# First transfers over two queues, four weight products at a time in an attention's last step, and a projection split around the first expert tile

## The chip, the core and the metric

The kernel runs on one core of one Trainium2 chip. A core has five engines that run their own instruction streams side by side and wait for each other by semaphores: TensorE (PE in the profile, with its weight loads as PEld), VectorE (DVE), ScalarE (ACT), GpSimd (POOL) and SyncE (SP, which here only issues transfers). The metric is the device time of one execution in microseconds (us), the median of several.

## What is computed

Two layers of cross attention and mixture of experts in float32, on x of 2 x 512 rows of 256 numbers, with a context of 2 x 1024 rows:

```python
x = x + L0_xattn(layernorm(x), ctx, ctx, mask0)      # 16 heads of 16; Wq, Wk, Wv, Wo with biases
x = x + L0_ffn(layernorm(x))                         # 8 experts 256-512-256, gelu, the best one of each row
x = x + L1_xattn(layernorm(x), ctx, ctx, mask1)      # layer norms of q, k and v with gains
x = x + L1_ffn(layernorm(x))                         # 7 experts 256-704-256, silu, two of each row, and a shared one
```

The attention of a head is softmax(q k^T / 4 + mask) v. The masks leave all but the last keys open in a way that lets the kernel compute with 256 keys of a batch instead of 1024 where a check on the masks (`flags`) allows it. That check is made on the chip, in the first half of layer 0's attention.

## The kernel before

**Start.** `sp_start` and `act_start` issue the first transfers on two queues, SP's and ACT's. SP's are the first half of x (tile `X`), the two halves of mask 0 (1 MB each), the second half of x, two bias rows, and mask 1. ACT's are the small constants (`cols`), the key weights (`WP` 0), the two halves of the context (`CT`), the value weights and the query weights. `pe_start` projects the keys as soon as the context and the key weights are there (L359, eight matmuls), then the first two of four value blocks (L380); then it transposes the normalized rows of x (L354), which DVE (`statistics`, L412 and what follows) and ACT (L451) make; then it projects the queries (L359 again), counts the open keys (L502), and goes on to the scores. POOL fills `KT` with a constant (L607), ACT fills `QT` in four pieces, two of them ahead of its copy of the keys out of PSUM (L637).

**An attention** has eight steps (`STEPS`; a step is a batch of 512 queries and a group of four heads), each of four gaps. In a gap of step n PE makes two of the eight *weights products* of the step (L859, keys by queries, 32 x 512 a matmul pair), whose exponentials ACT takes (L1201, PX), and two *tops*, the score products of a later step (L849), of which DVE takes the row maxima (L1039). Between the gaps stand the outputs (L880, twice a step, weights by values), the transposition of the maxima (L868), which DVE adds to the queries (L1045), and the transposition of a finished output (L893), which DVE divides (L1051, L1053). Tops use three PSUM banks in turn (`m_claim`), weights products three others (`e_claim`): a product waits until the one three before it is read. `pe_beside`, `dve_beside` and `act_beside` put other work into named gaps. In step 0 DVE works off `key_counts_rest` (L520 to L534) for mask 0, a piece after each top; in steps 2 and 3 the same for mask 1. SP starts to load the experts' weights behind the branch on `flags`, which DVE writes at the end of step 3.

**The last step** (7) has no tops. PE's order in it is: products 0 and 1, a transposed output, products 2 and 3, outputs, the transposition of the normalized rows of batch 0 (L354, written by DVE at L447 in step 6), products 4 and 5, in layer 0 the routing logits (L1520), products 6 and 7, a transposed output, outputs, in layer 0 the ranks (L1598 to L1603), outputs. In step 6 DVE makes the rows' statistics, one piece after each top.

**From attention to experts.** After the ranks DVE computes the places of the rows (`places0`), POOL scatters them to a buffer in HBM (L1688, four of batch 0), and SP reads tile 0 from it (L1813). Meanwhile PE (`fast_pe`) projects layer 1's keys and values from the context (L380, eight products each) and transposes batch 1's attention output (`close1`, L354). `ffn0_pe` runs over 16 tiles: transposing the next tile's rows (L1716, copied by DVE at L1785), up (L1730), down of the tile before (L1743), and `beside(i)`. `beside(0)` projects batch 1's output (`project1`, L380, 3.62 us); DVE adds it (L1060) and makes the statistics of the second rows, all in its own `beside(0)`. Batch 1's ranks stand in tile 4, and tile 8 waits for the scatter of batch 1. After the tiles comes layer 1's attention with the same steps, then the shared expert (L1855, L1866) and the routed ones (L1946, L1961).

## Time and profile before

| | us |
|---|---|
| median of 3 executions | 538.05 (535.56 to 538.39) |
| the profiled execution | 537.39 |
| its span, first to last instruction | 536.2 |
| PE busy in it | 496.9 |
| DVE, ACT, POOL busy | 260.2, 200.7, 87.3 |
| mean granted clock of TensorE | 0.986 |

The span falls into the start (to 29 us), layer 0's attention (to 127), layer 0's experts (to 227), layer 1's attention (to 313), the shared expert (to 382) and the routed ones (to 528). A busy PE isn't a PE at its peak: a product that waits for a bank or streams through a quarter of the array counts as busy as well. So the page's shares tell which engine matters, and the timeline of a stretch tells what ends its waits.

### The profile page before, as it was taken

How to read it: one execution, taken by the hardware profiler on the slowest of the kernel's cores; microseconds unless marked ns; L12 is line 12 of the kernel's file. 1: busy time of each engine (PE TensorE's matmuls, PEld its weight loads, DVE VectorE, ACT ScalarE, POOL GpSimd, SP SyncE). 2: the span in 40 equal slices, each digit the busy share in tenths (PEclk: the TensorE clock that was granted, in tenths of full speed). 3: DMA queues.
4: the chain of work that ended last, by engine and by line, in shares of the span. 5: the costliest groups of instructions: out<-in, count | busy, mean ns of one | idle time of the engine just before them, and what ended most of it. 6: DMA issues, size and time to landing. Idle time of an engine off the chain costs nothing.

```text
span 536.2 us, 8761 instructions
## 1 busy us (share of the span) xinstructions
PE 496.9 (93%) x3261; PEld 367.5 (69%) x3261; DVE 260.2 (49%) x775; ACT 200.7 (37%) x415; POOL 87.3 (16%) x125
## 2 busy tenths in 40 slices
PE   0999999999888989999999989999899999999995
PEld 0456545646788979755465436756799999999994
DVE  6457798664337365496677833351422222222220
ACT  2445655461345643454746632220222222222221
POOL 3134400003002020020000000047012212211222
PEclk9997999998999998999999999999999999999999
DMA  8521006997113121047000030039687667766712
GB/s 307 173 58 41 2 1 220 367 372 213 39 40 119 52 88 31 27 157 230 2 1 0 2 119 0 1 88 389 209 269 253 201 197 244 247 200 204 247 15 32
DMA packets 43367, 73.13 MB, mean 136 GB/s; under 512 B 3537, under 2 KB 33713, under 8 KB 43316
## 3 DMA queue, kind: packets, MB, share of 16 engines
q1 hardware_dynamic: 34564, 61.26, 33.8%
q0 software_dynamic: 4336, 6.75, 5.8%
q10 hardware_dynamic: 4416, 4.47, 2.7%
q8 instruction: 29, 0.48, 0.4%
q14 instruction: 22, 0.18, 0.1%
HBM read 56.35 MB, written 14.51 MB: 132 GB/s over the span
## 4 chain that ended last, share of the span: by engine, by line
PE 72%; DVE 13%; DMA 6%; issue 4%; ACT 2%; another core or an unknown queue 2%; POOL 1%; ACTq 0%; POOLq 0%; DVEq 0%
PE PS L1946 16%; PE PS L1961 9%; PE PS L849 8%; PE PS L859 7%; PE PS L1855 5%; DVE W L1039 4%; PE PS L880 4%; PE PS L380 3%; PE PS L1730 3%; PE PS L1743 3%; PE PS L1866 3%; PE PS L359 2%; DMA CT<-in_ctxT 2%; PE PS L354 2%
## 5 line engine op out<-in xcount | busy, mean ns | idle before, releaser
L1039 DVE TENSOR_REDUCE W<-PS 128x2 f32<-128x512 f32 x128 | 83.9, 686 | 37.2 <-PE PS L849 36.5
L1946 PE MATMUL PS<-PR,W 128*128 128x128 f32 x836 | 96.5, 275 | 0.0
L1946 PEld LDWEIGHTS PS<-PR,W 128*128 128x128 f32 x836 | 94.9, 192 | 0.1
L849 PE MATMUL PS<-W 32*128 32x256 f32 x512 | 84.2, 407 | 2.6 <-DVE W L1039 2.1
L859 PE MATMUL PS<-W 32*128 32x512 f32 x256 | 84.9, 655 | 0.9 <-ACT W L1201 0.7
L849 PEld LDWEIGHTS PS<-W 32*128 32x128 f32 x512 | 55.6, 188 | 25.3 <-issue 11.5
L1961 PE MATMUL PS<-W,PR 128*128 x228 | 52.5, 380 | 0.8 <-ACT PR L2662 0.8
L2713 POOL DMA_INDIRECT out<-PR,slots x19 | 29.7, 1563 | 129.6 <-ACT PR L2662 126.5
L1201 ACT ACTIVATE PR<-PS 128x512 f32<-128x512 f32 x64 | 35.2, 595 | 35.8 <-PE PS L859 35.6
L1961 PEld LDWEIGHTS PS<-W,PR 128*128 128x128 f32 x228 | 41.9, 190 | 6.1 <-issue 1.2
L1201 ACT ACTIVATE W<-PS 128x512 f32<-128x512 f32 x64 | 34.8, 594 | 25.1 <-PE PS L859 24.9
L1982 DVE TENSOR_TENSOR PR<-PR,PS 128x512 f32<-128x512 f32 x19 | 13.1, 688 | 59.7 <-PE PS L1946 59.7
L1855 PE MATMUL PS<-XT,W 128*128 128x512 f32 x88 | 40.1, 596 | 0.0
L859 PEld LDWEIGHTS PS<-W 32*128 32x128 f32 x256 | 25.9, 186 | 15.2 <-issue 6.0
L1730 PE MATMUL PS<-PR,W 128*128 128x128 f32 x256 | 32.3, 280 | 0.0
L1730 PEld LDWEIGHTS PS<-PR,W 128*128 128x128 f32 x256 | 30.9, 197 | 0.3 <-issue 0.3
L1743 PE MATMUL PS<-W,PR 128*128 128x256 f32 x128 | 31.1, 383 | 0.0
L1855 PEld LDWEIGHTS PS<-XT,W 128*128 128x128 f32 x88 | 16.2, 190 | 16.5 <-issue 16.1
L1773 ACT ACTIVATE PR<-PS,b1c 128x128 f32<-128x128 f32 x64 | 18.2, 366 | 23.1 <-PE PS L1730 20.2
L1743 PEld LDWEIGHTS PS<-W,PR 128*128 128x128 f32 x128 | 23.0, 190 | 3.4 <-issue 1.0
L1866 PE MATMUL PS<-W,PR 128*128 128x256 f32 x96 | 22.9, 381 | 2.1 <-DVE PR L1900 1.2
L1866 PEld LDWEIGHTS PS<-W,PR 128*128 128x128 f32 x96 | 18.0, 190 | 9.9 <-issue 5.8
(274 smaller groups left out, 588.4 us busy)
## 6 DMA issues: line engine op xcount, KB each, us to landing
W<-in_rguT SPq DMA_DIRECT2D x19, 1408.0 KB
W<-in_L_ffn_W SPq DMA_DIRECT2D x16, 512.0 KB, 9.6
...
```

The source lines that it names most:

```text
L849: m = pe.matmul(PS[:, bank, q * FK:(q + 1) * FK], QT[r:r + 32, g, c:c + 128], KT[r:r + 32, g, b * FK:(b + 1) * FK], start=True, stop=True)
L859: pe.matmul(PS[:, bank, :], KT[r:r + 32, g, b * FK + kb * 128:b * FK + (kb + 1) * 128], QT[r:r + 32, g, 512 * b:512 * (b + 1)], start=True ...
L880: m = pe.matmul(PS[32 * j:32 * j + 32, 6, :], VV[:, 2 * b + kb, h * VW:h * VW + 32], PX[s % 2][:, 4 * kb + j, :], start=(kb == 0), stop=(k ...
L1039: dve.tensor_reduce(NM[:, s % 2, q:q + 2, c], PS[:, m_bank(use), :].rearrange("p (q n) -> p q n", q=2), AX, ALU.max).then_inc(sem("m_free" ...
L1201: act.activation(PX[s % 2][:, HEADS_W[k], :], PS[:, e_bank(use), :], ACT.Exp).then_inc(sem("e_free"), 1)
L1730: m = pe.matmul(PS[:, up_bank(i), j * 128:(j + 1) * 128], W[:, o:o + 128], XS0[:, i % 2, k, :], start=(k == 0), stop=(k == 1))
L1743: pe.matmul(PS[:, bk, 0:D], HT0[:, i % 2, j, :], W[:, o:o + D], start=(j == 0), stop=False)
L1855: m = pe.matmul(PS[:, 2 * (n % 2) + w, :], W[:, k * 2 * F1 + o:k * 2 * F1 + o + 128], XT[:, k, 512 * b:512 * b + 512], start=(k == 0), sto ...
L1866: m = pe.matmul(half(4 + t // 2, t), HS[:, n % 2, t * 128:(t + 1) * 128], W[:, o:o + D], start=(j == 0 and t % 2 == 0), stop=(j == NJ1 - 1 ...
L1946: m = pe.matmul(PS[:, bank, j * 128:(j + 1) * 128], W[:, o:o + 128], XS[:, r % 2, k, :], start=(k == 0), stop=(k == 1))
L1961: m = pe.matmul(PS[:, 6, 0:D], HT[:, r % 2, j, :], W[:, bass.ds(slot * SLOT + o, D)], start=(j == 0), stop=(j == NJ1 - 1))
L2713: ins = pool.indirect_dma_start(out, off, YO[:, r % 2, :], None, compute_op=ALU.add)
```

## The change

Five things are changed.

- **First transfers.** Both queues carry half of x, half of the context and one set of weights ahead of a half of mask 0. The query weights stand behind a half mask on ACT's queue. The filling of `KT` goes from POOL to ACT, and all four fillings of `QT` come later on ACT. DVE makes the statistics of x first. PE's first value blocks come behind the transpositions of x.
- **Key counts.** `key_counts_rest` of mask 0 goes from step 0 to step 1 (the condition in `start_fast_dve`).
- **Last steps.** In step 7 of both layers four products are made in gap 0 and four in gap 2; two of each four take banks of the tops' ring, which is idle then. Layer 1's rows turn in the rings too.
- **Rows' statistics.** In step 6 of layer 0 they go by pieces of 2, 2, 1 and 4 behind the gaps' tops, and batch 1's are split between tiles 0 and 1.
- **Layer 0's last projection.** `project1` goes from behind tile 0's up products to ahead of them: one half before tile 0's transposition, one half right after it. Batch 1's ranks and places go from tile 4 to tile 3. PE has a new wait for `ranked`.

```diff
-    ROUTINGS = ((0, 0, 4, E0, 2), (0, 4, 4, E0, 5), (1, 0, 8, E1, 7))
+    ROUTINGS = ((0, 0, 4, E0, 0), (0, 4, 4, E0, 5), (1, 0, 8, E1, 7))
...
+    ROWS_TURN, LOGITS = (7, 1), (7, 2)
+    ROWS_BEGUN, ROWS_PIECES = 0, (2, 2, 1, 4)
...
+    def weights_of(n, gap):
+
+        if n == STEPS - 1:
+            return range(2 * gap, 2 * gap + 4) if gap % 2 == 0 else ()
+        return (2 * gap, 2 * gap + 1)
...
+        for use, n in E_USES.items():
+            if use[0] == "weights" and use[2] == STEPS - 1 and use[3] % 4 > 1:
+                bank = (m_bank(f"rows{use[1]}_0_1") + use[3] % 4 - 1) % 3
+            else:
+                bank, turn = 3 + turn % 3, turn + 1
+            banks[use], before[use], last[bank] = bank, last.get(bank, 0), n
+        return banks, before
...
     def sp_start():
-        sp.dma_start(X[:, 0:4, :], x_v[:, 0:4, :]).then_inc(sem("x0"), 16)
-        mask0 = A["mask0"].rearrange("(q p) n -> p q n", p=128)
-        for i in range(2):
-            sp.dma_start(m0i[:, 2 * i:2 * i + 2, :], mask0[:, 2 * i:2 * i + 2, :]).then_inc(sem(f"m0_{i}"), 16)
+        sp.dma_start(X[:, 0:2, :], x_v[:, 0:2, :]).then_inc(sem("x0"), 16)
+        load_keys0(sp, 0)
+        sp.dma_start(WP[:, 1, :, :], A["L0_xattn_WvT"].rearrange("(k p) n -> p k n", p=128)).then_inc(sem("wp_1"), 16)
+        load_mask0(sp, 0)
         sp.dma_start(X[:, 4:8, :], x_v[:, 4:8, :]).then_inc(sem("x1"), 16)
...
         act.dma_start(cols[:, :, :], A["cols"]).then_inc(sem("col"), 16)
-        load_keys0()
+        act.dma_start(X[:, 2:4, :], x_v[:, 2:4, :]).then_inc(sem("x0"), 16)
+        act.dma_start(WP[:, 0, :, :], A["L0_xattn_WkT"].rearrange("(k p) n -> p k n", p=128)).then_inc(sem("wp_0"), 16)
+        load_keys0(act, 1)
+        load_mask0(act, 1)
+        act.dma_start(WP[:, 2, :, :], A["L0_xattn_WqT"].rearrange("(k p) n -> p k n", p=128)).then_inc(sem("wp_2"), 16)
...
-        preset_queries(0)
-        preset_queries(1)
-        for f in range(2):
-            act.wait_ge(*at(0, "k_ps", f + 1))
-            act.activation(CP[:, 0, f, :], PS[:, f, :], ACT.Identity, bias=cols[:, C_COMPACT, 2 + f:3 + f]
-                           ).then_inc(sem("compact"), 1)
+        for j in range(2):
+            preset(KT[:, 2 * j:2 * j + 2, :], C_MAX)
+        keys_compact(0)
         act.wait_ge(sem("stats"), NORMS[True]["x0_0"])
...
-        act.wait_ge(sem("consts"), CONSTS + 1)
         for r in range(2):
             spread(act, KT, 0, r).then_inc(sem("kt"), 16)
-        preset_queries(2)
-        preset_queries(3)
+        for j in range(2):
+            preset(QT[:, 2 * j:2 * j + 2, 0:512], C_MASK)
...
-        for f in range(2):
-            queries_compact(f, f)
+        queries_compact(0, 0)
+        for j in range(2):
+            preset(QT[:, 2 * j:2 * j + 2, 512:1024], C_MASK)
+        queries_compact(1, 1)
...
-        pe.wait_ge(*at(0, "wp_1", 16))
-        values_pair(0)
         pe.wait_ge(sem("consts"), CONSTS)
         pe.wait_ge(*at(0, "xn", 4))
         for k in range(2):
             turn4(2 + k, [XN[:, j, :] for j in range(4)], k).then_inc(sem("turned"), 1)
+        pe.wait_ge(*at(0, "wp_1", 16))
+        values_pair(0)
         pe.wait_ge(*compact(0, 1))
...
+        settle(v, dve.memset(VR[:, 0:4 * VT], 1.0))
+        settle(v, dve.memset(ones16[:, :], 1.0))
+        dve.wait_ge(sem("x0"), 32)
+        whole(statistics(v, "x0_0", [X[:, t, :] for t in range(4)]))
...
-        for i in range(2):
-            dve.wait_ge(sem(f"m0_{i}"), 16)
-            dve.tensor_scalar(mu0[:, 2 * i:2 * i + 2, :], m0i[:, 2 * i:2 * i + 2, :], 0.0, None, ALU.not_equal
-                              ).then_inc(sem("mu0"), 1)
+        mask0_ones(0)
         dve.wait_ge(*at(0, "turned", 2))
         dve.tensor_copy(XT[:, 1, 0:512], PS[:, 3, :]).then_inc(sem("xt"), 1)
+        mask0_ones(1)
...
+    def project_half_batch(use, before, wi, b, j):
+
+        if j == 0:
+            claim_both(use)
+            taken(6, before)
+            taken(7, before)
+        filled(6 + j, project_half(6 + j, j, wi, b))
...
             if (n, gap) == (7, 1):
-                turn_rows(1, 0)
+                pe.wait_ge(*at(1, "rows", 4))
+                turn_ring("rows1_0", rows_for(1, 0))
...
+        if n == STEPS - 1:
+            for k in weights_of(n, gap):
+                pe_weights(l, n, k)
+            return
...
-            late = counts_rest(v, s - 2) if s > 1 else key_counts_rest(v, 0, mc[0][:, 0, :], mt[0]) if s == 0 else iter(())
+            late = counts_rest(v, s - 2) if s > 1 else key_counts_rest(v, 0, mc[0][:, 0, :], mt[0]) if s else iter(())
...
+        new_values(0)
         turn_batch("close1", rows_for(0, 1))
+        new_values(1)
+        project_half_batch("project1", "close1", 3, 1, 0)
+        pe.wait_ge(sem("ranked"), 1)
         pe.wait_ge(sem("nk_raw"), 2)
         pe.wait_ge(sem("nv_raw"), 2)
...
-            elif i == 4:
-                ranks_pe(1).then_inc(sem("ranks"), 1)
...
         def beside(i):
-            if i == 0:
-                project_batch("project1", "close1", 3, 1)
-            elif i == 2:
+            if i == 2:
                 pe.wait_ge(*at(0, "rows", 8))
                 turn_batch("rows0_1", rows_for(0, 1))
+            elif i == 3:
+                ranks_pe(1).then_inc(sem("ranks"), 1)
...
+        ffn0_pe(MAIN, beside, mid, first_maxima, lambda: project_half_batch("project1", "close1", 3, 1, 1))
...
-            dve_step(0, s, v, late)
-            whole(late)
+            dve_step(0, s, v, rows if s == 6 else empty, ROWS_PIECES if s == 6 else None)
+            if s == 5:
...
+        dve_xt("close1", 1)
         whole(gates0(v, 0))
...
+        add_projected("project1", 1, 0)
...
         def beside(i):
             if i == 0:
-                add_projected("project1", 1)
-                whole(statistics(v, "rows0_1", rows_of(1)))
+                for j in range(2):
+                    dve.wait_ge(sem(f"free{6 + j}"), USES[6 + j]["project1"])
+                for _ in range(5):
+                    next(second_rows)
+            elif i == 1:
+                whole(second_rows)
             elif i == 2:
                 dve_xt("rows0_1", 1)
...
-            elif i == 4:
                 dve.wait_ge(sem("ranks"), 2)
...
+        values_taken(0)
+        act_xt("close1", (6,), 1)
+        values_taken(1)
```

`load_keys0(q, b)` now loads one half of the context on queue q, `load_mask0(q, i)` one half of mask 0, `preset` fills a part of `KT` or `QT`, `mask0_ones(i)` converts one half of mask 0, and `keys_compact(f)` and `values_taken(n)` are the loops of before, one turn each.

ACT's queue and engine from the kernel's start, before and then after. `cols` are the constants, `WP` weights, `CT` context, `W<-in_mask` mask 0:

```order
L629 DMA cols<-in_cols 128x28
L680 DMA WP<-in_L_xattn_WkT 128x2x256
L682 DMA CT<-in_ctxT 128x2x256 x2
L683 DMA WP<-in_L_xattn_WvT 128x2x256
L684 DMA WP<-in_L_xattn_WqT 128x2x256
L666 ACT_TABLE_LOAD
L666 ACTIVATE W<-W,cols 128x1024 x2
L637 ACTIVATE W<-PS,cols 128x512 x2
L451 ACTIVATE PR<-X,NW 128x256 x2
```

```order
L647 DMA cols<-in_cols 128x28
L648 DMA X<-in_x 128x2x256
L649 DMA WP<-in_L_xattn_WkT 128x2x256
L706 DMA CT<-in_ctxT 128x2x256
L709 DMA W<-in_mask 128x2x1024
L652 DMA WP<-in_L_xattn_WqT 128x2x256
L687 ACT_TABLE_LOAD
L687 ACTIVATE W<-W,cols 128x1024 x2
L692 ACTIVATE W<-PS,cols 128x512
L472 ACTIVATE PR<-X,NW 128x256 x2
L692 ACTIVATE W<-PS,cols 128x512
L663 ACTIVATE XT<-PS 128x512
```

Half of x, half of the context and a half mask are on this queue now, and the other weights and the first half of the context have left it.

DVE in steps 0 and 1 of layer 0, before and after. TENSOR_REDUCE W<-PS are the maxima of tops, and the rows with fsum belong to the key counts:

```order
L1039 TENSOR_REDUCE W<-PS 128x2
L526 TENSOR_TENSOR fsum<-fsum 128x1
L527 TENSOR_SCALAR fsum<-fsum 128x1
L1039 TENSOR_REDUCE W<-PS 128x2
L529 TENSOR_SCALAR fsum<-fsum 128x1
L530 TENSOR_TENSOR fsum<-fsum 128x1
L534 COPY fsum<-fsum 128x1
L793 COPY b1c<-PS 128x32
L794 COPY wgs<-PS 128x24
L1039 TENSOR_REDUCE W<-PS 128x2 x2
L1045 TENSOR_TENSOR W<-W,PS 128x512
```

```order
L1080 TENSOR_REDUCE W<-PS 128x2 x3
L541 TENSOR_SCALAR W<-W 128x256
L542 TENSOR_REDUCE fsum<-W 128x1
L1080 TENSOR_REDUCE W<-PS 128x2
L544 TENSOR_TENSOR W<-W 128x256
L545 TENSOR_REDUCE fsum<-W 128x1
L1080 TENSOR_REDUCE W<-PS 128x2
L547 TENSOR_TENSOR fsum<-fsum 128x1
L548 TENSOR_SCALAR fsum<-fsum 128x1
L1080 TENSOR_REDUCE W<-PS 128x2
```

The rows of before are from step 0, those of after from the end of step 0 and step 1; ahead of them step 0 has nothing but six maxima, two copies and two maxima.

PE in step 7 of layer 0, before and after. W 128x512 are the products (L859, now L887), 32x512 the outputs, WGC the logits:

```order
L859 MATMUL PS<-W 128x512 x2
L893 MATMUL PS<-ident,W 128x128 x4
L859 MATMUL PS<-W 128x512 x2
L880 MATMUL PS<-PR,VR 32x512 x4
L354 MATMUL PS<-ident,W 128x128 x8
L859 MATMUL PS<-W 128x512 x2
L1520 MATMUL PS<-WGC,XT 128x8 x8
L859 MATMUL PS<-W 128x512 x2
L893 MATMUL PS<-ident,W 128x128 x4
L880 MATMUL PS<-W,VR 32x512 x4
```

```order
L887 MATMUL PS<-W 128x512 x4
L921 MATMUL PS<-ident,W 128x128 x4
L908 MATMUL PS<-PR,VR 32x512 x4
L375 MATMUL PS<-ident,W 128x128 x8
L887 MATMUL PS<-W 128x512 x4
L1558 MATMUL PS<-WGC,XT 128x8 x8
L921 MATMUL PS<-ident,W 128x128 x4
L908 MATMUL PS<-W,VR 32x512 x4
```

Eight products that stood in four pairs stand in two fours, the second of them ahead of the logits.

PE from layer 1's new values to tile 1's up products, before and after. WP,CT are new keys or values, WP,XT is `project1`, ident,PR a tile's transposition and PR,W its up products:

```order
L380 MATMUL PS<-WP,CT 128x256 x8
L354 MATMUL PS<-ident,W 128x128 x8
L1716 MATMUL PS<-ident,PR 128x128 x4
L1730 MATMUL PS<-PR,W 128x128 x8
L380 MATMUL PS<-WP,XT 128x256 x8
L1716 MATMUL PS<-ident,PR 128x128 x2
L1730 MATMUL PS<-PR,W 128x128 x8
```

```order
L401 MATMUL PS<-WP,CT 128x256 x4
L375 MATMUL PS<-ident,W 128x128 x8
L401 MATMUL PS<-WP,CT 128x256 x4
L401 MATMUL PS<-WP,XT 128x256 x4
L1754 MATMUL PS<-ident,PR 128x128 x2
L401 MATMUL PS<-WP,XT 128x256 x4
L1754 MATMUL PS<-ident,PR 128x128 x2
L1768 MATMUL PS<-PR,W 128x128 x8
L1754 MATMUL PS<-ident,PR 128x128 x2
L1768 MATMUL PS<-PR,W 128x128 x8
```

`project1` has left the place behind the first up products, and its halves stand around the first transposition.

## Rows read from the trace of the kernel before

**Rows 1.** The page: busy time of each engine, its share, instructions.
```profile
PE 496.9 (93%) x3261; PEld 367.5 (69%) x3261; DVE 260.2 (49%) x775; ACT 200.7 (37%) x415; POOL 87.3 (16%) x125
```

**Rows 2.** Transfers by queue (q1 SP, q10 ACT) in 5-12 us: packets, MB, share.
```profile
q1 hardware_dynamic: 659, 2.09, 76.0%
q10 hardware_dynamic: 654, 0.62, 26.6%
```

**Rows 3.** ACT's queue in 0-5 us, in 0-11 us and in 11-13 us.
```profile
q10 hardware_dynamic: 340, 0.22, 13.8%
...
q10 hardware_dynamic: 819, 0.67, 18.8%
...
q10 hardware_dynamic: 351, 0.34, 51.5%
```

**Rows 4.** Timeline of the start: start, length, engine, line, what, [idle before].
```profile
12.88 5.30 PE L359 MATMUL PS<-CT,WP 128*128 128x512 f32 x8 [12.88 <-DMA CT<-in_ctxT]
...
20.03 1.06 PE L354 MATMUL PS<-ident,PR 128*128 128x128 f32 x8
...
21.97 1.95 PE L359 MATMUL PS<-XT,WP 128*128 128x512 f32 x4 [0.88 <-DVE XT L762]
```

**Rows 5.** Timeline of step 0, layer 0: PE waiting, the first and last key counts.
```profile
44.16 0.28 DVE L520 TENSOR_SCALAR W<-W 128x256 f32<-128x256 f32 x1
...
47.16 0.76 PE L849 MATMUL PS<-W 32*128 32x256 f32 x1 [0.63 <-DVE W L1039]
...
48.28 0.15 DVE L534 COPY fsum<-fsum 128x1 f32<-128x1 f32 x1
```

**Rows 6.** Stretches: length; busy PE, PEld, DVE, ACT, POOL; PEclk, DMA share, GB/s.
```profile
44.00:48.00 4.00, 3.12 (x24) 2.33 (x22) 3.83 (x11) 2.77 (x5) 0.00 (x0) 0.86 0.00 1
48.00:52.00 4.00, 4.00 (x21) 2.74 (x22) 2.72 (x8) 2.14 (x3) 2.27 (x11) 0.50 0.00 0
...
120.00:124.00 4.00, 4.00 (x23) 2.31 (x26) 1.24 (x7) 1.51 (x3) 0.00 (x0) 0.75 1.09 337
124.00:128.00 4.00, 4.00 (x31) 1.75 (x24) 2.01 (x14) 0.71 (x2) 0.00 (x0) 0.83 0.98 262
```

**Rows 7.** Starts of steps 0, 1 and 2, and last outputs of steps 3 and 4.
```profile
42.50 0.69 PE L859 MATMUL PS<-W 32*128 32x512 f32 x1
...
54.39 0.48 PE L849 MATMUL PS<-W 32*128 32x256 f32 x1
...
64.25 0.48 PE L849 MATMUL PS<-W 32*128 32x256 f32 x1
...
83.16 1.06 PE L880 MATMUL PS<-W,VR 128*32 128x512 f32 x8
...
91.23 1.07 PE L880 MATMUL PS<-PR,VR 128*32 128x512 f32 x8
```

**Rows 8.** Timeline of step 7, layer 0, on PE; the second L880 is the last outputs.
```profile
113.30 1.13 PE L859 MATMUL PS<-W 32*128 32x512 f32 x4
...
123.37 1.94 PE L880 MATMUL PS<-W,VR 128*32 128x512 f32 x8
...
125.53 1.07 PE L880 MATMUL PS<-W,VR 128*32 128x512 f32 x8
```

**Rows 9.** Timeline of PE at tiles 0 to 2, layer 0's experts.
```profile
136.62 0.41 PE L1716 MATMUL PS<-ident,PR 128*128 128x128 f32 x2 [1.61 <-DMA PR<-scratch_x]
...
139.74 3.62 PE L380 MATMUL PS<-WP,XT 128*128 128x256 f32 x16
...
149.06 0.41 PE L1716 MATMUL PS<-ident,PR 128*128 128x128 f32 x2 [1.85 <-DVE PR L1785]
```

**Rows 10.** Timeline: PE at tile 8's transposition.
```profile
172.85 0.44 PE L1716 MATMUL PS<-ident,PR 128*128 128x128 f32 x2 [1.36 <-DMA PR<-scratch_x]
```

**Rows 11.** Timeline of step 7, layer 1: products 4 to 6, and the shared expert's start.
```profile
307.80 1.13 PE L859 MATMUL PS<-W 32*128 32x512 f32 x6
...
313.10 3.70 PE L1855 MATMUL PS<-XT,W 128*128 128x512 f32 x8
```

123 lines of the change are left out of this document (64 added, 59 removed).

## The prediction

> **What bounds the kernel now.** I read the page's busy times and its last chain first: PE is busy for 93% of the span, DVE for half of it [rows 1]. So a change pays where PE itself gets shorter, or where it waits, and nothing that DVE, ACT or POOL do beside a working PE counts. Where PE waits is told by the timeline's idle times. The stretches touched by the change have five such places: the start, where nothing runs on PE until the context has landed at 12.88 us [rows 4]; step 0 of layer 0, where PE waits for DVE [rows 5] and then runs at half the clock [rows 6]; step 7, where PE makes its products in pairs with ACT behind them [rows 8]; tile 0 and 1 of layer 0's experts [rows 9]; and tile 8 [rows 10]. All later stages follow by semaphores, so a gain at one place is carried on unless a transfer with its own time is met.
>
> **First transfers.** In 5 to 12 us the two queues moved 659 and 654 packets, but 2.09 and 0.62 MB: they take turns by packets, and SP's are the mask's long ones of 4 KB against ACT's of 1 KB [rows 2]. ACT's queue was at 340 packets after 5 us and at 819 after 11, which is 80 packets/us beside the mask; when SP too had short packets, in 11 to 13 us, it moved 351, 175 packets/us [rows 3]. The skill says the same (the Trainium skill, DMA: Bandwidth & Descriptors, section Queues, rings and completion order: an engine takes turns between queue rows at packet granularity), and by this rule a context that stands behind or beside the mask gets a fifth of the bytes; the trace agrees, with 0.62 of 2.71 MB.
>
> After the change ACT has to move the constants (128 packets), half x, key weights and half context (256 each), 896 in all, as many as before, which took until 11.4 us, 1.3 us ahead of the landing at 12.7. The difference is what runs beside them: SP has 768 short packets and then 256 of the mask, where it had 512 short and 512 long. At about 4.6 us SP is through with 512, and ACT has some 300 (340 less 0.4 us at its pace) [rows 3]. SP's other 256 short ones take 256 / 175 = 1.5 us and take ACT to 555; the 256 long ones take 256 / 80 = 3.2 us, to 9.3, and take ACT to 811; the last 85 take 0.5 us, to 9.8. With 1.3 us to the landing the context is there at 11.1 to 11.2 instead of 12.7: 1.6 us. The nearest other row is 175 packets/us without any mask beside it, 3.4 us for the 596 packets left at 4.6: landing at 9.3; with both queues at full pace from their first byte it would be 7.6, 5.3 us of gain. I take 11.2, since SP does reach its mask before ACT reaches its end.
>
> The keys take 5.3 us from there [rows 4], to 16.5. Before, ACT normalized its rows of x only behind both copies of the keys, and PE made two value blocks (1.9 us) meanwhile. Now the normalizing stands between the two copies: keys' first half done at 11.2 + 3.6, copy 0.7, rows 1.1, so the rows are there at 16.6 and PE transposes them at 16.7 instead of 20.03 [rows 4]. The value blocks come next (1.9) and hide the two copies of the transposed rows (0.6 + 0.7). The first queries start at 19.65 instead of 21.97 [rows 4]. The query weights stand behind a half mask on ACT's queue: 256 long and 256 short packets after 9.8 us are 3.2 + 1.5 us, landing near 16, in time. ACT's fillings of `QT`, two of 1.09 us, fit between 19.3 and the first queries' end at 21.6, and two more end 0.3 us ahead of the second queries. DVE's `mask0_ones` (1.2 each) is done by 19.7, ahead of the counts. So **2.3 us** go, between 1.6 (the keys alone) and 6.
>
> **Steps 0 and 1.** Step 0 lasts from 42.5 to 54.39, 11.9 us [rows 7]. Its counts take DVE 2.3 us between 44.16 and 48.43 [rows 5], 0.6 us of it between two maxima, so the three banks of tops run dry and PE waits; then it goes at half the clock, 1.2 GHz: all of 48 to 52 us and, by the mean of 0.86, the last 1.1 us ahead of it [rows 6]. Steps without counts show what it could be: the last outputs of steps 3 and 4 start 8.07 us apart [rows 7]. Step 0 has neither outputs of a step before (1.07) nor a transposed output (0.5), but a small job (0.5): 7.1 us. ACT's own work in it is 8 x 0.55 + 2 x 1.05 = 6.5. I take 7.7, a gain of 4.2. The counts now stand in step 1, which lasts 9.9 us [rows 7] with DVE at 6.9; 9.2 of 9.9 is tight, and step 2, which has counts and a division on DVE, is 0.9 us longer. I charge 0.9. Net **3.3 us**; if the clock falls all the same, 1.0.
>
> **Step 6.** The last top's maximum has two statistics ahead of it instead of three (0.35 us): **0.3 us**.
>
> **Step 7 of layer 0.** From 113.30 to the end of the last outputs at 126.6 it lasts 13.3 us [rows 8]. A pair of products takes 1.13 us, and in layer 1's step 7 three take 1.13 as well [rows 11], since each uses another quarter of the array's rows; four I put at 1.2. The new order by durations: products 1.2, transposed output 0.5, outputs 1.05, then the rows (written by DVE at 116.2) 1.05, to 117.25; products 1.15, logits 1.9, to 120.3; transposed output 0.6, outputs 1.05; ranks, for which DVE's six small operations (1.3) must be done at 121.6; outputs 1.07: 123.3 at full clock. ACT has 8 x 0.55 + 2 x 0.6 = 5.6 us between 114.5 and 120.1 and isn't late for the outputs. The skill warns of that (the Trainium skill, TensorEngine Tiling (Array Packing), section PSUM Bottleneck: once row tiles speed up the products, copying out of PSUM may bound); by it the step would be ACT's 5.6 us plus what stands ahead and behind, which still ends ahead of 123.3 here. Before, outputs took 1.94 instead of 1.07 late in the step [rows 8], with the clock at 1.2 GHz for some 3.4 us of 120 to 128 [rows 6], behind the logits. The logits stay, so I assume that this comes again, 1.3 us: **2.0 us** go, 3.3 without it, 0 if the fours go no faster than pairs.
>
> **Tile 0.** The places follow the ranks, the scatter the places, the read the scatter, so tile 0 lands 2.0 us earlier too: near 134.6 where PE took it at 136.62 after 1.61 us of waiting [rows 9]. PE's path from the step's end at 124.6 is: new keys 3.6, transposed output 0.5, half the values 1.8, `close1` 1.0, the other half 1.8, half a projection 1.8 (half of 3.62 [rows 9]): 135.1. So the waiting is filled. Then the first transposition 0.4, the other half 1.8, the second transposition 0.4: tile 0's up at 137.7, hardly earlier than before (138.0), but with no projection behind it. Tile 1's up stands at 139.9 instead of 143.4. The statistics, 4.3 us on DVE ahead of the copy for which PE waited 1.85 us [rows 9], are now 1.8 ahead of one copy and 2.4 ahead of the next, beside PE's 3.7 and more per tile, so that wait goes as well: tile 2's up at 144.0 instead of 149.3. That is 5.3 us, of which 2.0 are step 7's; with 0.3 for copies that come late once, **3.0 us**. DVE's new wait for the ranks in tile 3 has only the copy of tile 5 behind it, which PE asks for 4 us later. The wait for `ranked` ends with the places, 9 us ahead of PE's coming to it.
>
> **Tile 8.** Batch 1's places come some 2 us further ahead by their own move, so that the read of tile 8 lands at its own pace ahead of PE: **1.4 us** [rows 10], 0 if not.
>
> **Step 7 of layer 1.** From 302.9 to 313.10 [rows 11]. By the same durations: products 1.2, 0.5, outputs 1.05, rows 1.1, products 1.2, 0.6, then outputs at 308.8, and the last at 309.9, when ACT's eighth exponential is done (308.0 + 4 x 0.55 less its start): shared work starts at 311.0. **2.1 us**. The chain behind it (DVE, POOL's scatter) starts from PE's work and shifts along.
>
> **Sum.** 2.3 + 3.3 + 0.3 + 2.0 + 3.0 + 1.4 + 2.1 = 14.4 us. The profiled execution took 537.39, so 523.0 for one like it; the median shown is 538.05, 0.66 above, which gives 523.7. I say **523.4**.
>
> **The rivals.** (A) The mask doesn't hold up the context, since ACT's queue gets going before 4 us: the start gives 6.0 instead of 2.3, so 519.7. For it: 1 KB packets at full pace need only 5 us. Against it: rows 2. Chance 0.15; with it I put the case that the clock's fall in step 7 doesn't come again, 522.1 alone.
> (B) Step 0 keeps its wait or its half clock, the small job then being what holds PE: 2.3 us less, 525.7. For it: POOL and the two copies stand in the same gap; against: DVE would have only 5.8 us of work in 7.7. Chance 0.2.
> (C) The fours don't do what they say, since the banks borrowed from the other ring come free late: steps 7 give nothing, 4.1 us less, 527.5. Against it: three at once in rows 11. Chance 0.08.
> (D) The expert loads and the buffer's zeroing start with the branch and come only 5.6 us earlier, while the scatter comes 7.6 earlier and runs into the end of a backlog that kept the transfers' share near 1 until 128 us [rows 6]; tiles 0 and 8 then give 1 instead of 4.4: 526.8. Chance 0.1.
> (E) Slower: PE falls to half the clock more often. Two stretches of this attention spend over 5 and 3.4 us at 1.2 GHz [rows 6]. If thinner waits left it there through steps 1 to 6 (58 us, all PE), it would need 14.4 / 0.5 = 29 us at half clock to eat the gain; all of it would give 552. Chance 0.02.
>
> **How the numbers follow.** The forecast has 0.45. Its own terms move by the start (516 to 524) and by the clock. The range 516 to 529.5 takes in A to D and the bounds of each term. What a measurement of this kernel can tell from no change is about 0.5%, 2.7 us: only E and a sum of B, C, D and the low end of the start reach above 535.4. Faster 0.95, same 0.02, slower 0.03.
>
> **What would show it.** First keys at 11.2, first queries near 19.7, first top of step 1 near 48.8 with the granted clock at full through it; last outputs of step 7 some 7.6 us earlier; no idle time ahead of tiles 0, 2 and 8; layer 1's step 7 at 8.1 us. The prediction is wrong if the context lands after 12.5, if maxima still hold PE in step 0, or if ACT ends its exponentials after PE wants the outputs.

## The result, and the profile after

The changed kernel took 522.55 us (median of 4 runs, 519.58 to 523.77) against 537.82 us (4 runs, 535.56 to 538.39) of the kernel before: a ratio of 0.972, 95% interval 0.967 to 0.977. 523.4 us was predicted, with a range of 516.0 to 529.5. The profiled execution's span went from 536.2 to 522.5 us, by 13.7 us. The page of the changed kernel begins so, where [rows 1] stands before it:

```profile
PE 490.4 (94%) x3259; PEld 366.3 (70%) x3261; DVE 259.0 (50%) x776; ACT 201.1 (38%) x416; POOL 85.8 (16%) x124
```

PE is busy 6.5 us less and waits 7.2 us less. Where that is, the timelines of both traces tell: the start of the same piece of work in either, in us, with the shift that the prediction's terms had added up to by then.

| Work of PE | before | after | shift | predicted |
|---|---|---|---|---|
| first product of tops | 29.45 | 26.98 | -2.5 | -2.3 |
| step 1 of layer 0 | 54.39 | 48.14 | -6.3 | -6.5 |
| step 2 | 64.25 | 59.15 | -5.1 | -5.6 |
| step 7 | 113.30 | 108.03 | -5.3 | -5.9 |
| behind step 7's last outputs | 126.53 | 117.58 | -9.0 | -7.9 |
| tile 2's up | 149.30 | 136.73 | -12.6 | -10.9 |
| tile 7's up | 173.12 | 159.64 | -13.5 | -12.3 |
| step 7 of layer 1 | 302.92 | 289.42 | -13.5 | -12.3 |
| shared expert of layer 1 | 313.10 | 297.68 | -15.4 | -14.4 |
| first full up of a routed tile | 382.01 | 369.04 | -13.0 | -14.4 |
| last products | 527.68 | 514.03 | -13.7 | -14.4 |

So 15.4 us had been won by the shared expert, and 1.7 were given back behind it. Stretches in which PE's granted clock is 1.2 instead of 2.4 GHz have a part in this: ahead of the end, the trace of before has four times 1.7 us of such loss (twice in step 0, once in step 7, once at 200 us), that of the changed kernel two (at 187 and 364 us). So of the 13.7 us of this pair up to 3.4 are clock and at least 10.3 are not. The rows of the changed kernel's trace, in the order of the prediction's steps. First PE's timeline at the start (start, duration, then line, operation, count, and in brackets the idle time ahead and what ended it), which answers to [rows 4]:

```profile
10.98 6.40 PE L380 MATMUL PS<-CT,WP 128*128 128x512 f32 x8 [10.98 <-DMA CT<-in_ctxT]
17.22 1.04 PE L375 MATMUL PS<-ident,PR 128*128 128x128 f32 x8
19.82 1.88 PE L380 MATMUL PS<-XT,WP 128*128 128x512 f32 x4
26.98 1.14 PE L877 MATMUL PS<-W 32*128 32x256 f32 x8
```

The context is taken at 10.98 (11.2 predicted) and the first queries stand at 19.82 (19.65 predicted). The queues between 5 and 12 us, which answer to [rows 2] (packets, MB, share of the engines):

```profile
q1 hardware_dynamic: 663, 1.43, 52.9%
q10 hardware_dynamic: 696, 1.24, 47.5%
```

Again the two move the same number of packets, and now ACT's queue (q10) gets 1.24 MB of 2.67 instead of 0.62 of 2.71. Then step 0: PE's only wait in it, and the windows (PEclk is the granted clock, the third number from the end), which answer to [rows 5, 6]:

```profile
43.90 0.45 PE L877 MATMUL PS<-W 32*128 32x256 f32 x1 [0.37 <-DVE W L1080]
...
44.00:48.00 4.00, 4.00 (x36) 2.35 (x36) 3.10 (x8) 3.22 (x6) 2.46 (x12) 1.00 0.00 0
48.00:52.00 4.00, 4.00 (x36) 2.04 (x32) 3.24 (x8) 2.96 (x6) 3.42 (x12) 1.00 0.00 0
...
120.00:124.00 4.00, 4.00 (x26) 3.54 (x25) 1.59 (x4) 0.49 (x1) 3.09 (x4) 1.00 0.94 317
```

Step 0 lasts 8.1 us instead of 11.9, at full clock. Step 7 of layer 0, from its first four products to its last outputs, against [rows 8]:

```profile
108.03 1.14 PE L887 MATMUL PS<-W 32*128 32x512 f32 x8
...
112.93 1.95 PE L1558 MATMUL PS<-WGC,XT 128*128 128x8 f32 x16
114.74 0.64 PE L921 MATMUL PS<-ident,W 128*128 128x128 f32 x4
115.30 1.06 PE L908 MATMUL PS<-W,VR 128*32 128x512 f32 x8
...
116.59 1.06 PE L908 MATMUL PS<-W,VR 128*32 128x512 f32 x8
```

Eight records of 1.14 us in all are the four products (two matmuls each); a pair took 1.13 before. Tiles 0 to 2, against [rows 9]:

```profile
128.69 0.41 PE L1754 MATMUL PS<-ident,PR 128*128 128x128 f32 x2 [0.89 <-DMA PR<-scratch_x]
...
132.88 1.95 PE L1768 MATMUL PS<-PR,W 128*128 128x128 f32 x16
...
136.51 0.38 PE L1754 MATMUL PS<-ident,PR 128*128 128x128 f32 x2
```

Tile 1's up stands at 132.88, and the wait of 1.85 us for the copy is gone. Layer 1's step 7, against [rows 11], with a wait for ACT's exponentials at its end, and the place behind the shared expert where the late loss begins:

```profile
289.42 1.14 PE L887 MATMUL PS<-W 32*128 32x512 f32 x8
...
296.68 1.06 PE L908 MATMUL PS<-W,VR 128*32 128x512 f32 x8 [0.55 <-ACT W L1239]
...
363.36 0.92 PE L1906 MATMUL PS<-W,PR 128*128 128x256 f32 x3 [1.93 <-DVE PR L1940]
...
364.00:368.00 4.00, 4.00 (x14) 3.19 (x13) 1.49 (x6) 0.00 (x0) 0.00 (x0) 0.58 1.05 307
```

### The profile page after: what moved, and what is told of

Read it like the earlier page. It is cut to its first block, busy times and chain, and to the rows that moved or that the text cites. A ratio compares the mean times of both kernels' runs of the same rounds, so it can differ in the third digit from the quotient of the medians.

```text
span 522.5 us, 8762 instructions
## 1 busy us (share of the span) xinstructions
PE 490.4 (94%) x3259; PEld 366.3 (70%) x3261; DVE 259.0 (50%) x776; ACT 201.1 (38%) x416; POOL 85.8 (16%) x124
## 4 chain that ended last, share of the span: by engine, by line
PE 73%; DVE 12%; DMA 6%; issue 4%; ACT 2%; POOL 1%; ACTq 0%; SPq 0%; POOLq 0%; DVEq 0%
PE PS L1986 17%; PE PS L877 8%; PE PS L2001 8%; PE PS L1895 6%; PE PS L887 6%; PE PS L1906 4%; PE PS L908 3%; DVE W L1080 3%; PE PS L401 3%; PE PS L1768 3%; PE PS L380 3%; PE PS L1781 2%; PE PS L375 2%; DMA CT<-in_ctxT 2%; PE PS L896 2%
## 5 line engine op out<-in xcount | busy, mean ns | idle before, releaser
L887 PE MATMUL PS<-W 32*128 32x512 f32 x256 | 78.7, 638 | 0.2
L877 PEld LDWEIGHTS PS<-W 32*128 32x128 f32 x512 | 55.1, 184 | 24.8 <-issue 11.2
L887 PEld LDWEIGHTS PS<-W 32*128 32x128 f32 x256 | 24.0, 183 | 13.3 <-issue 6.6
L1781 PE MATMUL PS<-W,PR 128*128 128x256 f32 x128 | 31.0, 382 | 0.0
L1906 PE MATMUL PS<-W,PR 128*128 128x256 f32 x96 | 24.4, 399 | 2.9 <-DVE PR L1940 1.9
## 6 DMA issues: line engine op xcount, KB each, us to landing
W<-in_mask SPq DMA_DIRECT2D x2, 1024.0 KB, 12.6
```

The costliest lines, as they stand in the source:

```text
L877: m = pe.matmul(PS[:, bank, q * FK:(q + 1) * FK], QT[r:r + 32, g, c:c + 128], KT[r:r + 32, g, b * FK:(b + 1) * FK], start=True, stop=True)
L887: pe.matmul(PS[:, bank, :], KT[r:r + 32, g, b * FK + kb * 128:b * FK + (kb + 1) * 128], QT[r:r + 32, g, 512 * b:512 * (b + 1)], start=True ...
L1781: pe.matmul(PS[:, bk, 0:D], HT0[:, i % 2, j, :], W[:, o:o + D], start=(j == 0), stop=False)
L1906: m = pe.matmul(half(4 + t // 2, t), HS[:, n % 2, t * 128:(t + 1) * 128], W[:, o:o + D], start=(j == 0 and t % 2 == 0), stop=(j == NJ1 - 1 ...
```

## The experiments

Twelve more runs were made on three chips, of nine varied kernels and three repeats, each beside the kernel before on its own chip. Since stretches at 1.2 GHz turned out to come and go between executions of one kernel, the table takes them apart: "at half clock" is (1 - the mean granted clock of an execution) x its span, averaged over the runs; the rest, the mean time less that, is called the schedule here and set against the kernel before's on the same chip. The split is rough in three ways. A fall of the clock behind PE's last products is in every trace (0.2 to 1.7 us by this measure) and is taken off though it costs nothing. And a stretch inside counts in full though PE partly waits in it: the one in step 0 of the first trace of before counts 3.4 us, and the step is 2.6 us longer than in the second trace, which has none there. And the slow start of the keys (5.1 to 6.5 us until PE's next work, see the last section) isn't in the column, so it scatters the schedule.

| Kernel | runs | ratio to before (95%) | at half clock, us | schedule against before, us |
|---|---|---|---|---|
| before, on the three chips | 7, 13, 14 | 1 | 7.2, 7.4, 6.7 | 0 |
| changed, first | 4 | 0.972 (0.967 to 0.977) | 3.9 | |
| changed, again (after2) | 4 | 0.968 (0.965 to 0.971) | 1.4 | -10.9 |
| u_start | 4 | 0.979 (0.977 to 0.980) | 3.1 | -7.8 |
| u_counts | 4 | 0.973 (0.970 to 0.976) | 4.0 | -11.2 |
| u_pairs | 4 | 0.980 (0.977 to 0.983) | 3.4 | -7.4 |
| u_proj | 4 | 0.980 (0.976 to 0.985) | 4.4 | -7.7 |
| b_counts | 10 | 0.996 (0.993 to 0.998) | 4.2 | +1.0 |
| fours_only | 7 | 0.992 (0.989 to 0.995) | 7.2 | -4.8 |
| mask_last | 4 | 0.965 (0.962 to 0.969) | 2.1 | -13.4 |
| mask_last2 (the same) | 5 | 0.969 (0.966 to 0.973) | 2.2 | -12.3 |
| m_split | 6 | 0.970 (0.967 to 0.974) | 3.6 | -13.2 |
| m_counts0 | 6 | 0.974 (0.969 to 0.979) | 7.9 | -13.8 |

The schedule of one kernel's runs scatters by 0.4 to 1.6 us (standard deviation). With four to seven runs each, two entries of the last column differ clearly only when they are some 2 us apart on one chip, and more across chips. u_start, u_counts, u_pairs and u_proj ran on one chip; after2, mask_last and b_counts on the second; mask_last2, m_split, m_counts0 and fours_only on the third. So the undone kernels are best set against u_counts, whose only difference from the changed kernel leaves the schedule as it is in the traces (below): they are longer than it by 3.4, 3.8 and 3.5 us.

**The kernels once more.** after2 is the changed kernel, before2 the kernel before, both without an edit.

> The changed kernel once more, beside the others, to have its time and a second trace of it. If its steps are the program's, step 0 lasts 8.1 us, step 1 11.0, layer 0's step 7 9.5 and layer 1's 8.2, at full clock, as in the first trace; if they are one execution's, they differ. Open: whether PE again waits 1.93 us for the second to last chunk of the shared expert and then runs at 1.2 GHz for some 4 us, which cost 1.8 us in the first trace, and whether the stretch at 1.2 GHz behind the wait at 186 us comes again (2.3 us). With both it takes 0.9716 of the kernel before, without them 0.964.

> The kernel before once more, for a second trace. Theory (its falls of the clock are placed by its waits): 1.2 GHz again in step 0 behind the waits for DVE, in layer 0's step 7 behind the logits, and behind the wait for x1 at 200 us. Rival: only some of these places fall in any one execution, as the run with pairs, whose step 7 stayed at 1.00, lets suspect; then a second trace shows another set.

after2 took 519.46 us. Its trace has no stretch at 1.2 GHz ahead of the end, and the same distances: first tops at 27.32, last outputs of step 7 at 116.9 (0.3 behind the first trace in both). The wait behind the shared expert was 1.19 us. before2 took 537.37 us and had another set of stretches than the first trace. Its windows, columns as above:

```profile
36.00:38.00 2.00, 2.00 (x3) 0.74 (x3) 1.10 (x3) 0.00 (x0) 1.78 (x5) 0.50 0.08 26
48.00:50.00 2.00, 1.23 (x12) 0.80 (x7) 1.91 (x5) 1.72 (x3) 0.00 (x0) 1.00 0.00 0
122.00:124.00 2.00, 2.00 (x7) 0.54 (x4) 0.86 (x5) 0.44 (x1) 0.00 (x0) 0.50 1.09 336
126.00:128.00 2.00, 2.00 (x20) 0.49 (x16) 1.04 (x7) 0.00 (x0) 0.00 (x0) 0.50 0.97 328
```

Step 7 fell again and for longer, step 0 did not (PE waited in it the same 0.63 us for DVE, and the step took 9.3 us instead of 11.9), and there were stretches at 36, 241 and 309 us that the first trace hasn't. The starts of its step 0 and step 1:

```profile
45.40 0.69 PE L859 MATMUL PS<-W 32*128 32x512 f32 x1
...
54.67 0.48 PE L849 MATMUL PS<-W 32*128 32x256 f32 x1
```

So neither theory holds alone: step 7's is regular, the others come by chance, some more often than others.

**u_start: the first transfers undone.** All hunks of the diff from the order of transfers to DVE's start were put back; for instance

```diff
-        sp.dma_start(X[:, 0:2, :], x_v[:, 0:2, :]).then_inc(sem("x0"), 16)
-        load_keys0(sp, 0)
+        sp.dma_start(X[:, 0:4, :], x_v[:, 0:4, :]).then_inc(sem("x0"), 16)
+        mask0 = A["mask0"].rearrange("(q p) n -> p q n", p=128)
```

> The changed kernel with the order of first transfers, and of what ACT, DVE and PE do with them, put back as it was. Theory (the start's gain is real and carried to the end): the context lands at 12.7 to 12.9 us again, the first product of tops starts at 29.4 instead of 26.98, every later stage is 2.5 us later: 525.0 against 522.5. Rival (a later stage has a time of its own, so the start's gain would have been swallowed): the first tops at 29.4, but some wait later shorter by as much, 522.5.

It took 521.91 us against 533.54 of before. PE's timeline:

```profile
12.94 6.41 PE L380 MATMUL PS<-CT,WP 128*128 128x512 f32 x8 [12.94 <-DMA CT<-in_ctxT]
...
21.20 1.06 PE L375 MATMUL PS<-ident,PR 128*128 128x128 f32 x8
23.14 1.95 PE L380 MATMUL PS<-XT,WP 128*128 128x512 f32 x4 [0.88 <-DVE XT L783]
...
30.52 0.71 PE L870 MATMUL PS<-W 32*128 32x256 f32 x4 [0.26 <-issue]
```

The context comes 1.6 to 2.0 us later and the first tops 3.2 to 3.5 us later than in the two traces of the changed kernel; the schedule loses 3.1 us against after2 and 3.4 against u_counts on its own chip. The start's gain is real, carried to the end, and larger than the 2.5 of the first pair of traces: from the start of the keys to the next work of PE it is 5.1 us in the first trace of before, 6.25 here and 6.24 in the changed kernel. So the first pair understated it by a quick start of before, not by anything of the change. The wait of 0.88 us for the copy of the transposed rows is in the kernel before too and goes with the new order.

**u_counts, b_counts, m_counts0: the place of the key counts.** One condition moves them; u_counts takes them back to step 0 in the changed kernel, b_counts to step 1 in the kernel before, and m_counts0 back to step 0 beside mask_last.

```diff
-            late = counts_rest(v, s - 2) if s > 1 else key_counts_rest(v, 0, mc[0][:, 0, :], mt[0]) if s else iter(())
+            late = counts_rest(v, s - 2) if s > 1 else key_counts_rest(v, 0, mc[0][:, 0, :], mt[0]) if s == 0 else iter(())
```

> The changed kernel with the key counts back in step 0. Theory (the counts on DVE make PE wait in step 0 and the clock falls behind it): step 0 lasts 11.9 us instead of 8.1, step 1 9.9 instead of 11.0, with 1.2 GHz for some 5 us from about 45 us on: 2.6 us more, 525.1. Rival (the counts cost DVE's 2.3 us, but the fall of the clock has another cause and has gone with the earlier start): step 0 at 9.5, step 1 at 9.9, no half clock: 522.8.

> The kernel before with the key counts in step 1 instead of step 0, and nothing else changed. Theory: step 0 goes from 11.9 to 8.1 us with the clock at full, step 1 from 9.9 to 11.0: 2.6 us less than before. Rival (the half clock falls where it will, once or twice in any attention, and is only moved): step 0 at 8.1 to 8.5, step 1 at 11.0, and another stretch at 1.2 GHz elsewhere: 0.5 us less.

> The kernel with the mask behind, with the key counts whole in step 0. Theory (of the 3.8 us that step 0 gave in the first two traces, 1.3 were schedule, as step 1 gives 1.2 of it back, and the rest was a half clock that falls now here, now there): steps 0 and 1 together as long as with the counts in step 1, within 0.3 us, where the clock stays full; the median within 1.5 us of the kernel with the mask behind, with a mean clock lower by up to 0.003. Rival (the counts in step 0 are what makes the clock fall): a stretch at 1.2 GHz at 46 to 50 us in the trace, and 2.5 us more.

u_counts took 519.76 us (the kernel before on its chip 533.54), b_counts 533.75 (536.27) and m_counts0 524.09 (535.84). Windows of u_counts, of m_counts0 and of b_counts:

```profile
46.00:48.00 2.00, 2.00 (x13) 1.35 (x14) 1.76 (x3) 1.60 (x3) 1.44 (x7) 0.61 0.00 0
48.00:50.00 2.00, 2.00 (x18) 0.64 (x12) 0.65 (x2) 0.75 (x2) 1.41 (x7) 0.54 0.00 0
```

```profile
43.09 0.45 PE L877 MATMUL PS<-W 32*128 32x256 f32 x1 [0.63 <-DVE W L1080]
...
44.00:46.00 2.00, 2.00 (x10) 1.16 (x8) 1.29 (x5) 0.60 (x1) 0.89 (x5) 0.50 0.00 0
46.00:48.00 2.00, 2.00 (x12) 1.58 (x14) 1.38 (x2) 1.54 (x2) 1.43 (x8) 0.50 0.00 0
```

```profile
46.00:48.00 2.00, 1.62 (x19) 1.52 (x17) 1.48 (x4) 1.75 (x3) 0.00 (x0) 1.00 0.00 0
48.00:50.00 2.00, 2.00 (x22) 1.41 (x19) 1.58 (x3) 1.54 (x3) 1.47 (x7) 1.00 0.00 0
```

With the counts in step 0 the clock fell in it in 4 of 5 traces (before, u_counts, m_counts0, fours_only; not before2); with the counts in step 1 (m_split has half of them there) in none of 9. And in m_counts0 against mask_last2, on one chip, the half clock costs 5.7 us more (7.9 against 2.2; 4.7 more without m_counts0's longest execution), while the schedule is the same (-13.8 against -12.3). b_counts has 3.2 us less at half clock than before and a schedule 1.0 longer, which its trace doesn't show in these steps. In median time the move is worth 2.5 us on the kernel before (b_counts) and beside mask_last 4.4 by the medians and 2.5 by the ratios (m_counts0 against mask_last2; the ratio leaves out m_counts0's longest execution). Beside the changed kernel itself it is less clear: u_counts' ratio is 0.973 where the changed kernel's two are 0.972 and 0.968, so between 0.6 and 2.6 us with intervals that overlap, where 2.6 was expected. What there is of gain is clock: on the schedule, what step 0 wins (1.2 us where no clock falls, 9.3 against 8.1) step 1 gives back (9.9 against 11.0); both steps together take 19.1 us in before2 and in b_counts. The theory for m_counts0 was right in that, and wrong in holding that the falls go here and there: its rival, that the counts in step 0 bring the fall, was right, though not without exception (before2).

**u_pairs and fours_only: products in fours.** u_pairs takes the fours away and keeps the rest; fours_only keeps the fours, with the banks and the order that they need, the new place of the ranks and the pieces of step 6, and puts back all else.

```diff
-        if n == STEPS - 1:
-            return range(2 * gap, 2 * gap + 4) if gap % 2 == 0 else ()
         return (2 * gap, 2 * gap + 1)
...
-            if use[0] == "weights" and use[2] == STEPS - 1 and use[3] % 4 > 1:
+            if False:
```

> The changed kernel with the weights products of both last steps in pairs again, in their old banks. Theory (fours save their own durations, and the half clock in layer 0's step is the pairs' doing): layer 0's step 7 back from 9.5 to 13.2 us, layer 1's from 8.2 to 10.2, with 1.2 GHz for some 3 us behind the logits: 5.6 us more, 528.1. Rival (the half clock has nothing to do with pairs and fours, only the durations do): layer 0's step 11.5 us, 2.0 more there and 1.9 in layer 1: 526.4, with the clock at 1.00 throughout step 7.

> The kernel before with the fours of weights products in both last steps, their banks and the rows' turn through the ring, the new ranks' place and the statistics' pieces of step 6, but the old first transfers, the old place of the key counts, and the last projection behind tile 0's up. Theory (the fours pay 3.5 us by themselves, 1.6 in layer 0 and 1.9 in layer 1, and all three traces of the old step 7 show a half clock in it from 121 us on that the fours take away): 13.2 to 9.5 us in layer 0, 10.2 to 8.2 in layer 1: 5 to 6 us less than before, 0.990. Rival (the half clock there does not hang on pairs or fours, as the kernel with pairs and everything else new had none): it comes again at 116 to 124 us, and 3.5 us go: 0.9935.

u_pairs took 522.23 us (533.54), fours_only 532.04 (535.84). Of u_pairs one window and the last products of layer 0's step 7:

```profile
112.00:116.00 4.00, 4.00 (x29) 2.91 (x29) 0.99 (x3) 1.97 (x4) 0.00 (x0) 1.00 1.09 350
...
115.56 1.13 PE L885 MATMUL PS<-W 32*128 32x512 f32 x4
116.62 0.66 PE L919 MATMUL PS<-ident,W 128*128 128x128 f32 x4
117.20 1.06 PE L906 MATMUL PS<-W,VR 128*32 128x512 f32 x8
```

Of fours_only the window of step 7, and tile 0's transposition:

```profile
120.00:122.00 2.00, 2.00 (x21) 1.81 (x24) 0.49 (x3) 1.61 (x4) 0.00 (x0) 1.00 1.09 340
...
134.95 0.41 PE L1747 MATMUL PS<-ident,PR 128*128 128x128 f32 x2 [2.36 <-DMA PR<-scratch_x]
```

In pairs layer 0's step lasts 11.7 us (107.74 to 119.48), in fours 9.55. The fours' own worth is 2.2 us there and 1.9 in layer 1 (10.18 against 8.26); u_pairs' schedule is 3.5 us longer than after2's and 3.8 longer than u_counts'. Alone (fours_only) they give 4.8 us of schedule with the small edits beside them, and 3.8 of median. PE waits 2.36 us for tile 0 instead of 1.61 there: a part of step 7's gain is lost at the next wait, unless the projection fills it. The half clock of step 7 has been in all three traces with the old step in its old surroundings (before, before2, b_counts) and in none of the eleven others, the pairs of u_pairs among these. So it is regular and the traces of the changed step lack it, but it isn't the pairs by themselves. Nor does its going show in the mean: fours_only, whose trace has none there, still spends 7.2 us at half clock, as much as the kernel before (6.7), and its ratio, 0.992, stands between the theory's 0.990 and the rival's 0.9935. What about that step brings it stays open; what differs in u_pairs is the logits' bank, the pieces of step 6 and the surroundings.

**u_proj: the projection behind tile 0's up again**, with all statistics of its rows in one piece.

```diff
-        project_half_batch("project1", "close1", 3, 1, 0)
...
+            if i == 0:
+                for j in range(2):
+                    project_half_batch("project1", "close1", 3, 1, j)
...
+                whole(second_rows)
```

> The changed kernel with the last projection whole behind tile 0's up and the statistics of its rows in one piece behind it, as before; the values stay split around the transposition. Theory (projection and statistics behind tile 0's up are what PE waited for in tiles 0 and 1): tile 0 is waited for 1.6 us longer, and the copy for tile 2's up comes 1.85 us late again: 3.3 us more, 525.8. Rival (the waiting is the transfers' and is only moved): tile 0 is waited for longer, but tile 7's read, for which PE now waits 0.57 us, then lands in time, and the places for the second batch are no later: 1 us more, 523.5.

524.34 us (533.54). The waits of [rows 9] are back, 1.81 us for tile 0 where before had 1.61, and 1.85 for the later copy as before:

```profile
128.25 0.41 PE L1754 MATMUL PS<-ident,PR 128*128 128x128 f32 x2 [1.81 <-DMA PR<-scratch_x]
129.34 0.41 PE L1754 MATMUL PS<-ident,PR 128*128 128x128 f32 x2 [0.68 <-DVE PR L1824]
...
142.32 0.41 PE L1754 MATMUL PS<-ident,PR 128*128 128x128 f32 x2 [1.85 <-DVE PR L1824]
```

The schedule is 3.2 us longer than after2's, as the theory has it (3.3). By the ratios (0.980 against 0.972 and 0.968) the loss would be 4.5 to 6.4 us; this kernel also spent 4.4 us at half clock, 1.7 of it in the profiled run right behind the first two of these waits.

**mask_last: each half of the mask one transfer later.**

```diff
-        load_mask0(sp, 0)
         sp.dma_start(X[:, 4:8, :], x_v[:, 4:8, :]).then_inc(sem("x1"), 16)
+        load_mask0(sp, 0)
...
-        load_mask0(act, 1)
         act.dma_start(WP[:, 2, :, :], A["L0_xattn_WqT"].rearrange("(k p) n -> p k n", p=128)).then_inc(sem("wp_2"), 16)
+        load_mask0(act, 1)
```

> The changed kernel with each half of the mask one transfer later: on SP behind the second half of x, on ACT behind the query weights. Theory (queues take turns by packets, so the mask's 4 KB packets beside the context's 1 KB ones hold it up): the context lands 1.2 to 1.6 us earlier, at 9.4 to 9.8 instead of 10.9, first keys and first tops follow by 1.2, the mask still lands ahead of DVE's use of it at 18 us: 1.2 us less than the changed kernel. Rival (the first bytes are late, not the packets' turns): the context lands at 10.9 as before, and the mask, now last, makes the counts' products wait at 21.5: the same time or up to 1 us more.

> The kernel with the mask behind, once more, as the measure for the two that vary it. Its gain over the changed kernel is 2.0 to 2.6 us by the first trace (context at 9.15 instead of 11.35 us), so a ratio to the kernel before of 0.963 to 0.966; if the first time of it was lucky, 0.968 as the changed kernel.

517.04 us (536.27), and on another chip 519.65 (535.84). The queues between 5 and 9 us, first of mask_last, then of after2:

```profile
q10 hardware_dynamic: 678, 0.66, 52.7%
q1 hardware_dynamic: 657, 0.65, 48.4%
```

```profile
q1 hardware_dynamic: 428, 0.92, 62.4%
q10 hardware_dynamic: 486, 0.54, 38.0%
```

ACT's queue moves 170 packets/us where SP too has short ones, and 122 where SP's are partly the mask's long ones (0.92 MB in 428 packets). PE's timeline of mask_last:

```profile
9.15 6.27 PE L380 MATMUL PS<-CT,WP 128*128 128x512 f32 x8 [9.15 <-DMA CT<-in_ctxT]
15.26 1.04 PE L375 MATMUL PS<-ident,PR 128*128 128x128 f32 x8
...
18.04 1.96 PE L380 MATMUL PS<-XT,WP 128*128 128x512 f32 x4
...
25.28 1.14 PE L877 MATMUL PS<-W 32*128 32x256 f32 x8
```

The context lands 1.8 to 2.2 us earlier than in after2 and the first tops follow by 1.7 to 2.0, with no new wait. That the mask holds up the context is shown; the landing of 9.15 and 9.55 is where the prediction had put it for a queue with no mask beside it (9.3). As a time the gain is less certain: against after2 on its chip 2.4 us of median, with intervals that overlap; its ratios are 0.965 and 0.969, the changed kernel's 0.968 and 0.972. The schedule column (-13.4 and -12.3 against -10.9) points the same way, within its scatter; the earlier start is certain by the traces, the gain in the total is likely and not shown.

**m_split: half of the counts behind step 0's last top.**

```diff
+        own_counts = key_counts_rest(v, 0, mc[0][:, 0, :], mt[0])
         for s in range(4):
-            late = counts_rest(v, s - 2) if s > 1 else key_counts_rest(v, 0, mc[0][:, 0, :], mt[0]) if s else iter(())
-            dve_step(0, s, v, late)
-            whole(late)
+            late = counts_rest(v, s - 2) if s > 1 else own_counts
+            dve_step(0, s, v, late, None if s else (0, 0, 0, 2))
+            if s:
+                whole(late)
```

> The kernel with the mask behind, and of the key counts the first two pieces (1.85 us on DVE) behind the last top of step 0, the other two in step 1. Theory (step 1 is DVE's: 9.4 us of it in 11.0, and step 0 has 2 us of idle DVE): step 1 goes from 11.0 to 9.9, step 0 from 8.1 to 8.3: 0.9 us less than with the mask behind alone. Rival (step 1 is as long as PE's own work, the small counts job and ACT's copies make it): step 1 stays at 10.8 or more and step 0 gets longer: 0 to 0.5 us more.

520.21 us beside mask_last2's 519.65: inconclusive as a time. In its trace the outputs in step 1's second half stand at 55.37 where mask_last2 has 55.87, so 0.4 us of the expected 0.9 is there at most (first tops 0.1 apart); step 1 is mostly PE's own work and the small jobs.

## Why the prediction was right

**First transfers**, 2.3 us: right in the mechanism, and too small. The context at 10.98 was predicted to 0.2 us, and mask_last shows by the opposite edit that the turns by packets set it. The reading of the Trainium skill (DMA: Bandwidth & Descriptors, section Queues, rings and completion order: an engine takes turns between queue rows by packets) agrees with 122 packets/us beside the mask and 170 without. The term itself measures 3.1 to 3.4 us in the schedule and 3.2 to 3.5 in the traces. What I had from one trace alone was the keys' duration, 5.1 us to the next work there and 5.5 to 6.5 in the thirteen others, so that the 2.5 us of the first pair agree with 2.3 by luck; and the wait for the copy that u_start shows as 0.88 us was in neither of my terms by name.

**Steps 0 and 1**, 3.3 us: 2.6 in the first pair of traces (3.8 in step 0, 1.2 given back in step 1), and right by the median, but the reasoning stood on one leg only. I took the 4.2 us of step 0 as one thing. The runs split the 3.8 that came into 1.2 of schedule (before2's step 0 has no stretch in it and takes 9.3 us), which step 1 takes back whole, and 2.6 of a fall of the clock that comes in four of five traces with the counts in step 0. So the waits for DVE that the prediction counted are worth nothing over the two steps, and the clock, which it took for their companion, is the whole of the term. Rival B (the wait or the half clock stays, 525.7) didn't come as a time: 0.37 of the 0.63 us of waiting stayed, the half clock didn't.

**Step 7 of layer 0**, 2.0 us: 3.7. The order and the durations were right (9.55 us against 10.0 at full clock). The assumption that failed is that the half clock would come again because the logits stay; it came in none of the eleven traces with anything else of the change around that step. That case I had priced with 3.3 us and put into rival A. Rival C (fours no faster, 527.5) is refuted: four take 1.14 us. The Trainium skill's warning (TensorEngine Tiling (Array Packing), section PSUM Bottleneck: with the products sped up by row tiles, copying out of PSUM may bound) shows itself once, in layer 1, as 0.55 us of waiting for ACT, which with another 0.2 for DVE is why **step 7 of layer 1** gave 1.9 and not 2.1.

**Step 6**, 0.3 us: 0.2 in the traces (7.8 us in place of 8.0). The prediction's last section leaves this term out (7.6 us at step 7's last outputs, where its terms add up to 7.9).

**Tile 0**, 3.0 us: 3.6 in the traces and 3.2 by u_proj. The filling works, but tile 0 is still waited for, 0.89 and 1.25 us in the two traces, where I had none: it lands 12.1 us behind the start of the last outputs instead of 11.1. The delay stands between the end of POOL's scatter and SP's read: 1.46 us in before, 2.50 and 2.95 in the two traces of the changed kernel, 1.5 to 2.2 in the other new ones. It is 1.5 in the three traces where the scatter runs behind the full transfers (before, before2, b_counts), and in the changed kernel the scatter starts at 119 us beside transfer engines that are full until 122. This fits rival D (the scatter runs into the transfers' backlog), at 1 to 1.5 us instead of the 3.4 I had for it; no run varied the backlog alone.

**Tile 8**, 1.4 us: 0.9 by the first traces, since PE now waits 0.57 us for tile 7's read instead.

**Behind the shared expert**, 0 us: 1.7 lost in the first trace, not foreseen. PE's wait for DVE is 1.93 us where it was 1.18, and the clock falls behind it. In after2 the wait is 1.19 and no clock falls. In the twelve later traces it goes with the chip: 1.1 to 1.2 on the one of after2, b_counts and before2, 1.9 to 2.0 on the one of fours_only, mask_last2, m_split and m_counts0, and absent on the one of the four undone kernels (u_), where PE waits 0.9 to 1.9 us for a transfer a little later. So it isn't the change's. The sum was right by 0.7 us partly by luck: this loss stood against terms that came out 1.0 us larger together.

**The signs that it named.** The context landed in time and the clock stayed full through step 0. But maxima did still hold PE in step 0, for 0.37 us where it was 0.63; ACT did end its exponentials late in layer 1's step 7, by 0.55 us; and tile 0 was waited for. Held maxima and late exponentials are two of its three signs of being wrong. They came, at 0.4 and 0.6 us, too small to turn the sum, and the account of who waits for whom was too clean at these places.

**Clock.** Of the 16.8 us between the means of after2 and its kernel before, 10.9 are schedule and 6.0 fewer stretches at 1.2 GHz. Undone one by one, start, fours and projection are worth 3.1, 3.5 and 3.2 us of schedule and the counts nothing; the 1.1 us that are left for the small edits and what the parts do for one another are within the scatter. The prediction had 14.4 us and gave the clock 2.3 of them, by step 0. Rival E (the thinner waits bring the clock down more often) went the other way.
